# Ordering VectorE's dependent operations apart, and a mask product ahead of a wait, in a fused attention and expert kernel

## The reference

```python
h = einsum('bhid,oi,od->bho', x, weighted_sum, weight)        # image tokens
h = concatenate([h, txt], axis=1)
# attention over the batch axis: for each position, 8 tokens attend to each other, 16 heads of 16
q, k, v = split(layernorm(h) @ in_proj_weight.T + in_proj_bias)
attn = softmax(l2_normalize(q) @ l2_normalize(k).T * exp(min(logit_scale, log(100))))
h = h + (attn @ v * head_scale) @ out_w.T + out_b
# feed-forward part: within ONE token the 16 heads attend to each other
x = layernorm(h); hn = rmsnorm(x) * gamma1
q = hn @ Wq + bq;  k, v = split((hn @ Wdown + bdown) @ Wup + bup)
att = softmax(einsum('bthd,btgd->bthg', q, k) / 4)
x = x + einsum('bthg,btgd->bthd', att, v) @ Wo + bo
h2 = rmsnorm(x) * gamma2;  gate = softmax(h2 @ Wg + bg)       # 8 experts, all of them used
out = h + x + einsum('btd,edf,bte->btf', h2, We, gate)
```

## Time and profile before

| | |
|---|---|
| runs | 799.55 us median of 3 (798.84 to 803.93) |
| the profiled execution | 801.38 us, of which 799.3 us is the span from first to last instruction |
| busy, share of span | PE 93%, DVE 88%, POOL 51%, ACT 47% |
| granted TensorE clock | 0.981 of full on average |
| transfers | 33.25 MB, nearly all in the first 80 us |

### The profile page before, as it was taken

How to read it: one execution, slowest core, us unless ns; L and a number is a source line. 1 busy time by engine, 2 the same in 40 slices (tenths; PEclk the granted TensorE clock), 3 DMA queues, 4 the chain that set the end, 5 groups by cost and what they waited for, 6 DMA issues and landing times.

```text
span 799.3 us, 48197 instructions
## 1 busy us (share of the span) xinstructions
PE 745.6 (93%) x20274; PEld 508.0 (64%) x20274; DVE 703.5 (88%) x1591; ACT 374.4 (47%) x985; POOL 409.4 (51%) x1094
## 2 busy tenths in 40 slices
PE   4999978999999999876999999999999999999997
PEld 3888855666666666654656666666666666666553
DVE  5798778999999999765799999999999999999987
ACT  4478544665566665543333443344344434343321
POOL 1231355555666667444455665566556655665411
PEclk9999999999999999987899999999999999999999
DMA  9987000000000000000011001100111011101100
GB/s 331 326 252 228 3 3 4 2 0 0 0 0 0 0 0 2 11 17 10 15 26 28 23 16 26 26 23 16 26 26 26 14 26 26 26 13 27 29 16 20
DMA packets 38377, 33.25 MB, mean 42 GB/s; under 512 B 24786, under 2 KB 33570, under 8 KB 38314
## 3 DMA queue, kind: packets, MB, share of 16 engines
q1 hardware_dynamic: 38314, 32.35, 13.4%
HBM read 22.64 MB, written 4.83 MB: 34 GB/s over the span
## 4 chain that ended last, share of the span: by engine, by line
PE 39%; DVE 10%; issue 3%; DVEq 0%
PE bank L204 9%; PE bank L205 8%; PE bank L206 8%; PE bank L957 5%; PE bank L946 5%; DVE acc L1099 3%; DVE smax L1108 2%; PE bank L964 1%; DVE res L1099 1%; PE bank L977 1%; PE bank L1016 1%; PE bank L1003 1%; PE bank L1002 1%; DVE fq_t L1147 1%; DVE logits L1117 1%
## 5 line engine op out<-in xcount | busy, mean ns | idle before, releaser
L1099 DVE SCALAR_TENSOR_TENSOR acc<-bank,gate,acc 128x256 f32<-128x256 f32 x222 | 106.1, 478 | 12.8 <-PE bank L206 4.1
L204 PE MATMUL bank<-we_h,h_t_h 128*128 128x512 f16 x296 | 113.0, 382 | 3.7 <-DVE res L1099 1.0
L205 PE MATMUL bank<-we_l,h_t_h 128*128 128x512 f16 x296 | 112.2, 379 | 0.6 <-issue 0.6
L206 PE MATMUL bank<-we_h,h_t_l 128*128 128x512 f16 x296 | 112.2, 379 | 0.0
L204 PE MATMUL bank<-tokw_h,x_t_h 128*128 128x256 f16 x256 | 71.0, 277 | 11.3 <-DVE x_t_l L682 11.3
L1053 ACT ACTIVATE junk<-x 128x256 f32<-128x256 f32 x37 | 15.4, 417 | 120.4 <-DVE x L1143 120.4
L205 PE MATMUL bank<-tokw_l,x_t_h 128*128 128x256 f16 x256 | 70.9, 277 | 0.0
L206 PE MATMUL bank<-tokw_h,x_t_l 128*128 128x256 f16 x256 | 70.8, 277 | 0.0
L1188 POOL TENSOR_TENSOR t<-ss,rms_ws 128x1 f32<-128x1 f32 x37 | 7.1, 192 | 117.1 <-ACT junk L1053 117.1
L287 PE MATMUL bank<-vaug,pr_t 32*32 32x17 f32 x4736 | 49.8, 181 | 10.7 <-issue 10.7
L957 PEld LDWEIGHTS bank<-pr_t,v 32*32 32x32 f32 x4736 | 47.6, 104 | 18.7 <-issue 18.3
(11 more groups left out here) (223 smaller groups left out, 2232.8 us busy)
## 6 DMA issues: line engine op xcount, KB each, us to landing
xbuf<-in_x SPq DMA_DIRECT2D x32, 512.0 KB, 5.3
out<-res SPq DMA_DIRECT2D x36, 128.0 KB
we_s<-in_we SPq DMA_DIRECT2D x4, 512.0 KB, 7.3
inw<-in_in_w SPq DMA_DIRECT2D x1, 768.0 KB, 11.6
hn_t_h<-hn_r_h SPq DMA_TRANSPOSE x37, 2.3
hn_t_l<-hn_r_l SPq DMA_TRANSPOSE x37, 2.4
wrep<-in_w_rep SPq DMA_DIRECT2D x1, 512.0 KB, 4.8
h_all<-in_txt SPq DMA_DIRECT2D x1, 512.0 KB
```

The costliest lines, as they stand in the source:

```text
L204: nc.tensor.matmul(dst, a_h(c), b_h(c), start=start and c == 0, stop=False)
L205: nc.tensor.matmul(dst, a_h(c), b_l(c), start=False, stop=False)
L206: last = nc.tensor.matmul(dst, a_l(c), b_h(c), start=False, stop=stop and c == chunks - 1)
L1099: op = nc.vector.scalar_tensor_tensor(out=(res if e == E - 1 else acc)[:, :], in0=b_we[s % 2][:, k * D:(k + 1) * D], scalar=gate[p][:, e:e ...
```

## The change

In `attn_pe` the mask product goes ahead of the wait for `a_qkt` (except at tile 0), with a wait for `a_qkm` in front of it. In `attn_dve` `rsum` moves up from behind `pr_t` to behind `on_l`. In the feed-forward part the layouts of `fq_t` and `kv_t` change, so that DVE writes `fq_t` contiguously, and both operands of the score products are read with a step of 16 elements (64 bytes); the mask and the view of `b_o3` follow. `gate` becomes a `scalar_tensor_tensor`. `combine` now does one expert per call, and its eight calls are spread between other operations.

```diff
@@ attn_pe, body
-                    pe.wait_ge(a_qkt, i + 1)
+                    first = isinstance(i, int) and i == 0
+                    if first:
+                        pe.wait_ge(a_qkt, i + 1)
                     wait(pe, a_sub, i)
+                    pe.wait_ge(a_qkm, i + 1)
                     nc.tensor.matmul(b_s[:, :], am[:, 0:P], am[:, P:], start=True, stop=True,
                                      skip_group_check=True)
+                    if not first:
+                        settle(pe, c_in)
+                        pe.wait_ge(a_qkt, i + 1)
                     scores(range(0, 4))
@@ attn_dve, body
+                if real(i, -1):
+                    dve.wait_ge(a_av, i)
+                    nc.vector.reciprocal(rsum[:, :], o3[:, :, HD:HD + 1]).then_inc(a_rsum, 1)
                 if real(i, -3):
                     added(i - 3)
                 if real(i, 0):
                     dve.wait_ge(a_exp, i + 1)
                     nc.vector.transpose(pr_t[p][:, :, :], pr[:, :, :]).then_inc(a_prt, 1)
-                if real(i, -1):
-                    dve.wait_ge(a_av, i)
-                    nc.vector.reciprocal(rsum[:, :], o3[:, :, HD:HD + 1]).then_inc(a_rsum, 1)
@@ tiles and ffn_pe, scores
-        kv_t = sb("kv_t", [P, H, 32])
+        kv_t = sb("kv_t", [P, 32, 16])
...
-                                                fq_t[q, 2 * pair:2 * pair + 2, :].rearrange("r t h -> r (t h)"),
-                                                kv_t[q, :, 2 * pair:2 * pair + 2],
+                                                fq_t[q, :, pair],
+                                                kv_t[q, :, pair],
@@ ffn_dve, combine(i, p, e): one expert
+                s, k = divmod(e, EP)
+                if k:
+                    dve.wait_ge(f_acc, (i - 2) * STEPS + s + 1)
                 else:
-                    dve.wait_ge(f_comb, (i - 2) * STEPS + s)
...
+                    dve.wait_ge(f_we, (i - 2) * STEPS + s + 1)
+                    if s:
+                        dve.wait_ge(f_comb, (i - 2) * STEPS + s)
...
@@ ffn_dve, body (the layouts and the gate)
-                    nc.vector.tensor_scalar(gate[p][:, :], gexp[:, :], grec[:, :], r2[p][:, :], ALU.mult,
-                                            ALU.mult).then_inc(f_gmul, 1)
+                    nc.vector.scalar_tensor_tensor(out=gate[p][:, :], in0=gexp[:, :], scalar=r2[p][:, :],
+                                                   in1=grec[:, :].to_broadcast([P, E]), op0=ALU.mult,
+                                                   op1=ALU.mult).then_inc(f_gmul, 1)
...
-                    nc.vector.transpose(fq_t[:, :, :].rearrange("r t h -> r h t"), qpad[:, :, :])
+                    nc.vector.transpose(fq_t[:, :, :].rearrange("r (h t) p -> r h (t p)", t=2), qpad[:, :, :])
...
-                    nc.vector.transpose(kv_t[:, :, :], b_kv[:, :]).then_inc(f_kvt, 1)
+                    nc.vector.transpose(kv_t[:, :, :].rearrange("r n p -> r (n p)"), b_kv[:, :]).then_inc(f_kvt, 1)
...
-                                        kv_t[:, :, :].rearrange("r g (p t) -> r p g t", t=2)).then_inc(f_qt, 1)
+                                        kv_t[:, :, :].rearrange("r n p -> r p n")).then_inc(f_qt, 1)
...
-                    nc.vector.transpose(of[:, :, :], b_o3[:, :].rearrange("r (t h) -> r h t", h=H)).then_inc(f_of, 1)
+                    nc.vector.transpose(of[:, :, :], b_o3[:, :].rearrange("r (p h t) -> r h t p", h=H, t=2)).then_inc(f_of, 1)
```

More of the change, by code:

```diff
@@ L1082, in ffn_dve, with combine @@
         def ffn_dve(dve):
-            def combine(i, p, s):
+            def combine(i, p, e):
                 if not real(i, -2):
                     return
[L1087 to L1090, removed]
-                else:
-                    dve.wait_ge(f_comb, (i - 2) * STEPS + s)
[L1093 to L1102, removed]
+                s, k = divmod(e, EP)
+                if k:
+                    dve.wait_ge(f_acc, (i - 2) * STEPS + s + 1)
+                else:
+                    dve.wait_ge(f_we, (i - 2) * STEPS + s + 1)
+                    if s:
+                        dve.wait_ge(f_comb, (i - 2) * STEPS + s)
+                    else:
+                        dve.wait_ge(f_gmul, i - 1)
+                        dve.wait_ge(p_hx2, i - 1)
+                if e == E - 1:
+                    wait(dve, out_done, (i - 2) * 16)
+                nc.vector.scalar_tensor_tensor(
+                    out=(res if e == E - 1 else acc)[:, :], in0=b_we[s % 2][:, k * D:(k + 1) * D],
+                    scalar=gate[p][:, e:e + 1], in1=(acc if e else hx2[p])[:, :], op0=ALU.mult,
+                    op1=ALU.add).then_inc(f_comb if k else f_acc, 1)
@@ L1104, in body @@
             def body(i, p, middle=None):
+                s3 = b_s3[:, :].rearrange("p (h m) -> p h m", m=32)
                 if real(i, 0):
                     dve.wait_ge(f_s, i + 1)
-                    s3 = b_s3[:, :].rearrange("p (h m) -> p h m", m=32)
                     nc.vector.tensor_reduce(smax[:, :], s3, AX.X, ALU.max).then_inc(f_max, 1)
[L1109 to L1112, removed]
@@ L1118, in body @@
                                                    op0=ALU.mult, op1=ALU.add).then_inc(f_logit, 1)
+                if real(i, 0):
+                    dve.wait_ge(f_max, i + 1)
+                    wait(dve, f_exp, i)
+                    nc.vector.tensor_tensor(sc[:, :, :], s3, smax[:, :].unsqueeze(2).to_broadcast([P, 16, 32]),
+                                            ALU.subtract).then_inc(f_sub, 1)
+                if real(i, -2):
                     dve.wait_ge(f_logit, i - 1)
                     nc.vector.tensor_reduce(gmax[:, :], logits[:, :], AX.X, ALU.max, negate=True).then_inc(f_gmax, 1)
-                combine(i - 1, 1 - p, 3)
+                combine(i - 1, 1 - p, 6)
+                if real(i, -1):
+                    dve.wait_ge(f_onh, i)
+                    nc.vector.tensor_tensor(fon_l[:, :, :], b_turn[:, 0:D], fon_h[:, :, :], ALU.subtract).then_inc(f_onl, 1)
+                combine(i - 1, 1 - p, 7)
                 if real(i, 0):
@@ L1125, in body @@
                     nc.vector.transpose(pr_t[1][:, :, :], pr[:, :, :]).then_inc(f_prt, 1)
-                if real(i, -1):
-                    dve.wait_ge(f_onh, i)
-                    nc.vector.tensor_tensor(fon_l[:, :, :], b_turn[:, 0:D], fon_h[:, :, :], ALU.subtract).then_inc(f_onl, 1)
                 if real(i, -2):
@@ L1132, in body @@
                     dve.wait_ge(f_grec, i - 1)
-                    nc.vector.tensor_scalar(gate[p][:, :], gexp[:, :], grec[:, :], r2[p][:, :], ALU.mult,
-                                            ALU.mult).then_inc(f_gmul, 1)
+                    nc.vector.scalar_tensor_tensor(out=gate[p][:, :], in0=gexp[:, :], scalar=r2[p][:, :],
+                                                   in1=grec[:, :].to_broadcast([P, E]), op0=ALU.mult,
+                                                   op1=ALU.mult).then_inc(f_gmul, 1)
                 combine(i, p, 0)
+                if real(i, 1):
+                    dve.wait_ge(f_qpad, i + 2)
+                    nc.vector.transpose(fq_t[:, :, :].rearrange("r (h t) p -> r h (t p)", t=2), qpad[:, :, :])
                 combine(i, p, 1)
@@ L1166, in body @@
                                             ALU.subtract).then_inc(f_h2l, 1)
+                combine(i, p, 5)
                 if real(i, 0):
@@ L1301 @@
         "ident_c": np.eye(P, dtype=np.float32),
-        "amask_c": mask(4, lambda n: n % 32 // B, lambda n: n % 32 // B), "fmask_c": mask(2, lambda n: n % 32 // 16, lambda n: n % 2),
+        "amask_c": mask(4, lambda n: n % 32 // B, lambda n: n % 32 // B), "fmask_c": mask(2, lambda n: n % 2, lambda n: n % 2),
         "bv": columns(a["L0_attn_in_proj_bias"][2 * D:]), "bo": a["L0_ffn_bo"], "bq": a["L0_ffn_bq"], "bg": a["L0_ffn_bg"],
```

8 lines of the change are left out of this document (5 added, 3 removed).

## The result

| | before | after |
|---|---|---|
| median | 800.19 us (798.84 to 803.93, 4 runs) | 813.85 us (811.13 to 820.2, 4 runs) |
| ratio, 95% interval | | 1.0154 [1.0103, 1.0206] |
| profiled execution / its span | 801.4 / 799.3 | 820.2 / 818.1 |
| granted clock, mean | 0.981 | 0.967 |

The kernel became slower by 1.5%, where I had forecast 783 us. The profiled execution is the longest of the four, with the lowest mean clock (0.967; the other three have 0.975 to 0.981), so I compare stretches and tiles at the full clock rather than whole spans.

The account below looks back on a forecast made before the run. DVE was taken to set attention's pace; in the feed-forward part PE and DVE were balanced, PE stalling before expert step 1. Terms -8.4 - 7.5 - 1 = -16.9 us took the median 799.55 to about 783; range 776 to 801.

Parts of the forecast that it names:

- The scores' operands on PE: Feed-forward score products on PE: stepped reads taken at 0, upper bound 0.74 us a tile, +27 us over 37 tiles.
- Rival A: Stepped operands slow PE's score products; in full 810 us, chance 0.16; at part of its price about 796, chance 0.10.
- The chain to `res`: Feed-forward, from `smax` to the end of expert 7: 2.64 us against 2.89; term -7.5 us, bounds -8.8 and -2.
- the stall: Feed-forward: PE's wait for `res` before expert step 1, 0.26 us a tile; nearly all given back, 0.22 on 34 tiles.
- Rival C: Interleaving on DVE does nothing; only the shorter `fq_t` is left, off the path: 798 us, chance 0.03.
- `rsum`: Attention on DVE: moving it up cuts `sc` to `on` from 2.28 to 2.04 us, 0.24 less.
- the stage: Attention: both edits together save 0.27 us a tile over 31 tiles, -8.4 us, bounds -9.6 and -4.
- The mask product: Attention on PE: going first takes 0.32 us off the scores' path, of which only 0.06 a tile gains.
- the added waits: Attention on PE: waits on its own past product and a loaded constant, costed at nothing, bounded by 0 and 0.1 a tile.
- I take it as free in steady tiles: Attention on DVE: moved `rsum` waits for the previous tile's sums; no cost, as three DVE operations, about 1.6 us, pass between.
- The mixed stretch: Where attention and feed-forward share the engines: -1 us, between -5 and +3, clock effect not worked out.
- the list of chances: Whole kernel: faster by over 1% (below 791.6 us) 0.64, within 1% 0.20, slower 0.16.

Follow-up runs that it names:

- e1: Kernel before with only the new layouts of `fq_t` and `kv_t`, the mask and the view of the sums: 825.09 us against 801.83, ratio 1.0303.
- e4: Kernel before with only the new DVE order in the feed-forward part and the new `gate` operation: 790.98 us, ratio 0.9882.
- e3: Kernel before with both attention edits only (mask product ahead, `rsum` moved up): 801.83 us, ratio 0.9996.
- e7: Kernel before with only the mask product moved ahead of the wait for the keys: 807.08 us, ratio 1.0046.
- e9: Kernel before with only `rsum` moved up: 794.24 us, ratio 0.9919.
- e13: Changed kernel with the old layouts and the mask product behind its wait as before, `rsum` still moved up everywhere: 783.25 us, ratio 0.9780.
- e2: Changed kernel with the old layouts put back, everything else of the change kept: 789.54 us, ratio 0.9849.
- e12: Repeat of e2 (changed kernel with the old layouts), against the kernel before: 786.15 us, ratio 0.9834.
- e14: Kernel before with the mask product ahead in the loop's turns only (tiles 4 to 31): 803.80 us, ratio 1.0023.
- e10: Kernel before with both attention edits in the loop's turns only, the turns written out unchanged: 794.37 us, ratio 0.9941.
- e11: Changed kernel with the old layouts and both attention edits in the loop's turns only: 784.49 us, ratio 0.9815.

## Why the prediction was wrong

**The step that failed** is "The scores' operands on PE. This is the cost without a row", where I took 0. It measured 2.03 - 1.29 = 0.74 us a tile, the upper bound that I had worked out from DVE's writes, to which I had given a chance of 0.16. All of it lands on PE, which had no slack in the feed-forward part. e1 gives +24 us for it alone. Rival A in full, 810, was the outcome; its break-even of 1.75 us for the 128 products was passed by 0.28.

The arguments for 0 were bad ones. That pairs are free says nothing of single elements, which touch twice as many places for the same data. The stepped read of DVE that I used as the nearest row (`of`) reads a PSUM bank, not SBUF. And a stream that takes 0.88 ns a column "anyhow" doesn't hide the step: a stepped column takes 1.8 ns. The rule of the Trainium skill (Advanced Engine Details and Errata, SBUF Cachelines) that lines are 16 bytes, with at least two accesses needed in each, made the right distinction. The trace now agrees on both its sides: 8-byte pairs take 1.29 us, lone 4-byte elements 2.03. That a line has 16 bytes no run here tests.

**Right, by its own steps.** The chain to `res`: 2.60 us for 2.64, the stall gone, -9.4 us in e4 for -7.5. The term was a little low: tiles went from 11.39 to 11.11, 0.28, where I had counted 0.22 of the stall's 0.26, and its lower bound (-8.8) was passed, within e4's interval. Rival C, that the interleaving does nothing, falls with e4. `rsum`: 2.02 us for 2.04, and the tile 6.08 for 6.10. `fq_t` at 0.70, `gate` at 0.23 for 0.22 in the kernel after. `v48` costs 0.33 (1.04), the upper bound again, and is hidden, as I said it would be even then: DVE now waits about 2 us a tile.

**Wrong in attention.** I took -8.4 for the stage; e3 measured 0 (0.9996), of which steady tiles are -6.9. The mask product was worth 0.03 a tile where I had 0.06. That "the added waits" cost "nothing, bounded by 0 and 0.1 a tile" failed outside steady tiles: +3.7 us by e7, whose profiled execution has nearly all of its loss before tile 7. I had reasoned from one steady tile and multiplied by 31. "I take it as free in steady tiles" was true of `rsum`'s new wait, and e9 has it at -6.5 us.

**The mixed stretch** was put at -1, between -5 and +3. e3 loses 1.6 from tile 32 on, within the bounds; the clock there was 0.80 after for 0.86 before, 0.88 in e3, 0.92 in e4 and 0.85 in e13. e2 and e12, one kernel, have 0.93 and 0.87, so it follows no edit that I could name.

**The sum, redone** with what was measured: attention 0, feed-forward order -9.4, layouts +24: 799.55 + 14.6 = 814. Measured: 813.85 by the median, and 812 by the ratio 1.0154. That the sum meets the median to a fraction of a us is luck: the terms are uncertain by 3 to 5 us each, and the two gains are worth 9.4 us as measured apart but 12 to 13 as measured together (e2, e12). In the list of chances, 0.64 and 0.20 should read 0.63 and 0.21.

**What stays open.** Why the mask product ahead costs some 3 us. Its runs have longer stops inside the sums of line 287 (5.6 us in e7 for 3.0), but e14 has not (3.1), and e10's are longer than before (3.9) without a loss. The stops lie only in the turns written out and in the loop's first passes, so in code that is new to the engine, which fits PE's instructions arriving late; that is argued and not shown, since no row names what is being waited for. The falls of the clock come after such idle stretches, though not after every one, so how much of a late tile 7 is the stop and how much the clock isn't shown.

## What to carry to other kernels

A cost with no row and a wide upper bound does not belong at zero when it falls on the engine with no slack: put it at the bound, or leave the strided access to the engine that has time to spare. Here that is DVE: in e4 and e13 it writes `fq_t` with a step, 0.34 us more, and PE is busy for 338 to 339 us of 340 all the same. Ask of a "nearest row" whether it reads the same memory with the same run of bytes. And cost an edit separately for the steady turns and for those written out at the start: `steady gain times number of tiles` was right by tile and wrong by stage. And before a few us are placed in a stretch of one execution, compare its granted clock with that of the others.

## What the runs showed of the hardware

- A float32 element read or written alone, 64 bytes from the next in SBUF, has one price in all four places: PE's products 0.74 us for 1024 elements (0.72 ns more each), in the moving operand, the stationary one or both; DVE 0.34 to 0.37 us for 512, reading (1.04 for 0.69) or writing (1.04 for 0.70 of `fq_t`, 1.06 for 0.69 of `kv_t`), 0.66 to 0.72 ns more each. In the records of single products four start every 33 ns before and every 57 ns after (medians), with 32 columns each: 1.8 ns a column. Since four of 64 columns in order (line 297) start every 56 ns, a stepped column costs about as much as two in order.
- Two elements together (8 bytes) cost nothing, on PE (33 ns for four products, as for those of line 957 with both operands in order) as on DVE (`v48` at 0.69 to 0.71), and single elements read with a step from a PSUM bank by DVE cost nothing either (`of` at 0.67 to 0.71; `kv_t`, which reads its bank in order, 0.67 to 0.70).
- On DVE an operation that does not need the one before starts 0.08 us before that one ends, one that needs it 0.03 after. `gate` on 128x8 took 0.29 us as a `tensor_scalar` with two scalars and 0.23 as a `scalar_tensor_tensor`, but in some tiles around 0.46 before and around 0.6 in e2, e4, e11, e12 and e13, for no reason that I found.
- PE's granted clock falls to half after some stretches in which PE is mostly idle (0.23 us busy of 2 in e14), and the 64 products of a tile's attention scores then take 1.93 us instead of 1.09.
